# A fused mixture-of-experts and ternary feed-forward block on one core: one-hot tables from ScalarE, a first unit worked in column halves, reordered loads, and one last store

## The reference

```
x = x + tanh(g_xattn) * experts(layernorm(x), token_ids, ctx)
x = x + tanh(g_ffn)   * bitffn(layernorm(x), gate_w, gate_b, val_w, val_b, out_w, out_b)

experts: expert e = min(token_id // 6250, 3) of each row; per row
         y = (silu(h @ ctx[e].T) * (h @ ctx[e].T)) @ ctx[e].T   # one 512x512 matrix per expert, used three times
bitffn:  bit_linear = round(x * 127/max|x|) * max|x|/127  times  clip(round(w/mean|w|), -1, 1) * mean|w|, plus bias
         out = bit_linear(silu(bit_linear(x, gate)) * bit_linear(x, val), out_w)      # 512 -> 2048 -> 512
```

## Time and profile before

| What | us |
|---|---|
| median of 3 runs (309.02 to 309.77) | 309.68 |
| the profiled execution, whole | 310.04 |
| its span on the core | 308.3 |
| TensorE busy | 291.8 (95%) |
| VectorE busy | 261.4 (85%) |
| GpSimd busy | 238.5 (77%) |
| ScalarE busy | 219.2 (71%) |

### The profile page before, as it was taken

One profiled execution on the slowest core, in us unless ns is written; L12 is line 12 of the kernel. 1 busy time (PEld: TensorE's weight loads), 2 busy tenths in 40 slices (PEclk: granted clock), 3 DMA queues, 4 the chain that ended last, 5 costly groups with the idle time before them and its releaser, 6 DMA issues.

```text
span 308.3 us, 5341 instructions
## 1 busy us (share of the span) xinstructions
PE 291.8 (95%) x1438; PEld 141.0 (46%) x1439; DVE 261.4 (85%) x496; ACT 219.2 (71%) x276; POOL 238.5 (77%) x261
## 2 busy tenths in 40 slices
PE   1989999999999999999889999999999999999994
PEld 1445555544444555444334444444444444444453
DVE  5899987787988968679998999999998899888982
ACT  4959686777887746677986796668866876675650
POOL 5656854788888979936678799998989887977863
PEclk9999999999999999999999999999999999999999
DMA  6685798759997873923043635764445423543142
GB/s 261 228 314 202 271 313 305 251 120 307 336 279 189 230 218 102 292 60 109 19 92 72 121 69 119 122 151 88 107 115 119 85 68 86 119 87 82 54 102 105
DMA packets 58902, 49.10 MB, mean 159 GB/s; under 512 B 51135, under 2 KB 51135, under 8 KB 56576
## 3 DMA queue, kind: packets, MB, share of 16 engines
q1 hardware_dynamic: 54304, 35.43, 45.1%
q0 software_dynamic: 4576, 13.40, 12.5%
HBM read 28.35 MB, written 10.00 MB: 124 GB/s over the span
## 4 chain that ended last, share of the span: by engine, by line
PE 83%; DVE 7%; DMA 3%; issue 2%; POOL 2%; ACT 2%; DVEq 0%; POOLq 0%
PE banks L632 27%; PE banks L705 17%; PE banks L726 17%; PE banks L714 16%; PE banks L639 2%; DMA raw<-raw 2%; PE banks L609 1%; DMA xg<-in_x,gather_at 1%; DVE turned L1053 1%; DVE raw L1207 1%; DVE raw L1202 1%; POOL w_both L476 1%; DVE gu_sb L1102 1%; POOL out L548 1%; PE banks L745 1%
## 5 line engine op out<-in xcount | busy, mean ns | idle before, releaser
L476 POOL TENSOR_TENSOR w_both<-raw 128x1024 f32<-128x1024 f32 (+1 forms) x32 | 74.9, 2342 | 7.7 <-DVE raw L1202 6.8
L632 PE MATMUL banks<-w_both,turned 128*128 x348 | 80.0, 379 | 0.6 <-ACT turned L861 0.5
L939 ACT ACTIVATE w_both<-w_both,magic,raw 128x1024 f32 (+1 forms) x31 | 38.2, 1234 | 35.5 <-DVE raw L1221 35.5
L705 PE MATMUL banks<-tern,raw 128*128 128x512 bf16 x256 | 60.5, 379 | 1.6 <-DMA raw<-raw 1.2
L714 PE MATMUL banks<-tern,raw 128*128 128x512 bf16 x256 | 60.5, 379 | 1.3 <-DVE raw L1194 1.3
L726 PE MATMUL banks<-tern,xg 128*128 128x512 bf16 x240 | 56.1, 379 | 0.7 <-DVE raw L1230 0.7
L632 PEld LDWEIGHTS banks<-w_both,turned 128*128 128x128 f16 x348 | 34.0, 98 | 37.5 <-issue 2.3
L1194 DVE SCALAR_TENSOR_TENSOR raw<-banks,raw 128x1024 f32<-128x1024 f32 x32 | 40.8, 1276 | 4.7 <-issue 4.5
L1202 DVE SCALAR_TENSOR_TENSOR raw<-banks,raw 128x1024 f32<-128x1024 f32 x32 | 40.9, 1278 | 3.6 <-PE banks L714 3.6
L1207 DVE TENSOR_REDUCE raw<-w_both 128x1 f32<-128x1024 f32 x32 | 38.8, 1212 | 3.1 <-POOL w_both L476 2.9
L705 PEld LDWEIGHTS banks<-tern,raw 128*128 (+1 forms) x256 | 24.9, 98 | 32.1 <-DMA raw<-raw 1.4
(11 more groups left out here) (134 smaller groups left out, 420.2 us busy)
## 6 DMA issues: line engine op xcount, KB each, us to landing
raw<-in_ctx SPq DMA_DIRECT2D x4, 1024.0 KB, 6.7
raw<-in_L_ffn_gate_w SPq DMA_DIRECT2D x4, 1024.0 KB, 6.8
raw<-in_L_ffn_val_w SPq DMA_DIRECT2D x4, 1024.0 KB, 7.5
raw<-in_L_ffn_out_w SPq DMA_DIRECT2D x4, 1024.0 KB, 6.1
raw<-x_low SPq DMA_DIRECT2D x8, 257.5 KB, 3.5
raw<-x_high SPq DMA_DIRECT2D x8, 257.5 KB, 3.4
raw<-in_L_ffn_gate_b SPq DMA_DIRECT2D x1, 1024.0 KB, 5.4
raw<-in_L_ffn_val_b SPq DMA_DIRECT2D x1, 1024.0 KB, 9.5
```

The lines of the kernel that those rows point to most:

```text
L476: nc.gpsimd.tensor_tensor(z[:, t % 2, 2 * D * c:2 * D * c + width], g_sb[:, c, 0:width], v_sb[:, c, 0:width], ALU.mult).then_inc(z_made, 1)
L632: last = nc.tensor.matmul(acc[:, :], a[:, k * P:(k + 1) * P], flat(w[:, bass.ds(e4 + k, 1), :]), start=(k == 0 and i == 0), stop=(k == KD ...
L705: last = nc.tensor.matmul(ring[pair][:, b, :], flat(xiT[:, bass.ds(t % 2, 1), k, :]), tern[:, k * HC + 2 * c + b, :], start=(k == 0), stop ...
L939: nc.scalar.activation(zq[:, a:b], flat(z[:, bass.ds(t % 2, 1), a:b]), ACT.Identity, scale=flat(sc[:, bass.ds(t, 1), 12:13]), bias=magic[: ...
```

## The change

- One-hot tables: ScalarE spreads `iota_minus` and `iota_id` into two fp16 tables (`minus_rows`, `ids`) while it waits for the weights; their two iotas are made first on GpSimd. VectorE then makes `row_hot` with two `tensor_tensor` compares of 8 columns each on fp16 operands, laid out [place, column], so that a weight load of L595 takes every 16th element. The row number is multiplied into `unit_hot` instead. GpSimd's three compares are gone. The work for `experts_ready` now stands before the wait for the small matmuls.
- Unit 0: normalise, transpose, high half and low half each in two column halves, in two PSUM banks; the first product's first two matmuls need only the first half. `keep_warm(3)` becomes `keep_warm(1)`. ScalarE's second copy of weights comes earlier, since it uses one of those banks.
- SP: weight pieces 8 and 9 are loaded before the DMA transposes start, 10 and 11 behind the first and the third. The biases are loaded when `signed` is 12, not 16.
- Scales: the two x scales become one ScalarE instruction behind `x_round`; z's output scale is made by ScalarE (`out_scale`); z's floor of 1e-5 is a constant column behind z that `z_max` reads, so one VectorE step is gone.
- The end: one store of whole rows in place of two of half rows.

```diff
@@ -29,6 +29,7 @@
+    ZROW = H + 8
...
@@ -39,14 +40,13 @@
-    HOT_DVE = 13
+    HOT = (0, 8, COLS)
-    out_halves = out.rearrange("b s (c d) -> (b s c) d", c=2)
...
@@ -130,7 +129,9 @@
-        row_hot = turned[:, :, :].rearrange("p a b -> p (a b)").rearrange("p (c r) -> p c r", r=P)
+        minus_rows = tern[:, 0:4, :].bitcast(f16).rearrange("p g d -> p (g d)").rearrange("p (r c) -> p r c", c=COLS)
+        ids = tern[:, 4, 0:COLS * UNITS].bitcast(f16).rearrange("p (c u) -> p c u", c=COLS)
+        row_hot = turned[:, :, :].rearrange("p a b -> p (a b)").rearrange("p (r c) -> p r c", c=COLS)
...
@@ -152,7 +153,7 @@
-        x_frees = 6
+        x_frees, bias_frees = 6, 12
...
@@ -160,7 +161,7 @@
-        z = area(2 * H).rearrange("p (b d) -> p b d", b=2)
+        z = area(2 * ZROW).rearrange("p (b d) -> p b d", b=2)
...
@@ -178,6 +179,8 @@
+        first_hT = hT_ps[:, 0:D // 2], guT_ps[:, 0:D // 2]
...
@@ -305,11 +310,14 @@
+            load_weights(8)
+            gathers_landed(10)
+            load_weights(9)
-                if 8 + i < 12:
-                    load_weights(8 + i)
+                if i in (0, 2):
+                    load_weights(10 + i // 2)
...
@@ -321,7 +329,7 @@
-            sp.wait_ge(signed, G)
+            sp.wait_ge(signed, bias_frees)
...
@@ -342,14 +350,15 @@
-                sp.wait_ge(stored[n], 16 * ((TILES - 2 - n) // YS + 1))
-            for n in range(2):
-                sp.wait_ge(stored_last[n], 16)
+                sp.wait_ge(stored[n], 16 * TILES // YS)
+            for ap, pattern, first, step in ((iota_minus, [[-1, P]], 0, 0), (iota_id, [[1, COLS]], 1, COLS)):
+                nc.gpsimd.iota(ap, pattern=pattern, base=first, channel_multiplier=step,
+                               allow_small_or_imprecise_dtypes=True).then_inc(rows_counted, 1)
...
@@ -360,8 +369,7 @@
-            for ap, pattern, first, step in ((iota_unit, [[P, UNITS]], 0, 0), (iota_id, [[1, COLS]], 1, COLS),
-                                             (iota_place, [[P, UNITS]], 0, 1), (iota_minus, [[-1, P]], 0, 0)):
+            for ap, pattern, first, step in ((iota_unit, [[P, UNITS]], 0, 0), (iota_place, [[P, UNITS]], 0, 1)):
...
@@ -476,11 +484,7 @@
-            pool.wait_ge(consts32, 10)
-            pool.wait_ge(rows_named, 1)
-            for c in range(HOT_DVE, COLS):
-                nc.gpsimd.tensor_scalar(row_hot[:, c, :], iota_minus, minus_row[:, c:c + 1], iota_id[:, c:c + 1],
-                                        ALU.is_equal, ALU.mult).then_inc(hot_pool, 1)
+            pool.wait_ge(consts32, 8)
...
@@ -497,6 +501,7 @@
+                    nc.gpsimd.memset(z[:, :, H:H + 1], 1e-5).then_inc(z_floor, 1)
...
@@ -533,21 +538,13 @@
-                pool.wait_ge(o_made, t + 1)
+                pool.wait_ge(o_made, t + 2 if t == TILES - 1 else t + 1)
-            def store_last(c):
-                pool.wait_ge(last_named, 1)
-                pool.wait_ge(o_made, TILES + c)
-                nc.gpsimd.indirect_dma_start(
-                    out=out_halves, out_offset=bass.IndirectOffsetOnAxis(ap=half_row[:, c:c + 1], axis=0),
-                    in_=x1_in[:, (TILES - 1) % XR, c * D // 2:(c + 1) * D // 2], in_offset=None).then_inc(stored_last[c], 16)
...
@@ -568,10 +565,8 @@
-            for t in range(TILES - 4, TILES - 1):
+            for t in range(TILES - 4, TILES):
-            for c in range(2):
-                store_last(c)
...
@@ -588,11 +583,9 @@
-                if c < HOT_DVE:
-                    pe.wait_ge(hot_made, c + 1)
-                else:
-                    pe.wait_ge(hot_pool, c - HOT_DVE + 1)
-                last = nc.tensor.matmul(perm_ps, row_hot[:, c, :], unit_hot[:, c, :],
+                if c in HOT:
+                    pe.wait_ge(hot_made, HOT.index(c) + 1)
+                last = nc.tensor.matmul(perm_ps, row_hot[:, :, c], unit_hot[:, c, :],
...
@@ -629,6 +622,8 @@
+                        if experts == 1 and i == 0 and k == KD // 2:
+                            pe.wait_ge(hThi_made, 1)
...
@@ -661,6 +656,8 @@
+                    elif isinstance(j, int) and j == 0:
+                        pe.wait_ge(hThi_half, 1)
...
@@ -678,11 +675,17 @@
-            turn_h(0)
-            keep_warm(3)
+            for half, made, done in ((0, h_half, hT_half), (1, h_made, hT_done)):
+                pe.wait_ge(made, 1)
+                for k in range(KD // 2):
+                    last = nc.tensor.transpose(first_hT[half][:, k * P:(k + 1) * P],
+                                               h_of(0)[:, (half * KD // 2 + k) * P:(half * KD // 2 + k + 1) * P], ident32[:, :])
+                last.then_inc(done, 1)
+            keep_warm(1)
+                pe.wait_ge(hTlo_half, 1)
...
@@ -804,6 +807,9 @@
+            act.wait_ge(rows_counted, 2)
+            nc.scalar.activation(ids, iota_id.unsqueeze(2).broadcast_to([P, COLS, UNITS]), ACT.Copy).then_inc(tables_made, 1)
+            nc.scalar.activation(minus_rows, iota_minus.unsqueeze(2).broadcast_to([P, P, COLS]), ACT.Copy).then_inc(tables_made, 1)
...
@@ -832,9 +838,9 @@
+            w_copy(1)
-            w_copy(1)
...
@@ -848,6 +854,12 @@
+                    return
+                if j == 0:
+                    for half, done, made in ((0, hT_half, hThi_half), (1, hT_done, hThi_made)):
+                        act.wait_ge(done, 1)
+                        nc.scalar.activation(hT_of(0)[0][:, half * D // 2:(half + 1) * D // 2], first_hT[half], ACT.Copy,
+                                             scale=H_SCALE).then_inc(made, 1)
...
@@ -923,6 +935,8 @@
+                nc.scalar.activation(flat(sc[:, bass.ds(t, 1), 3:5]), gam[:, 0:2], ACT.Copy,
+                                     scale=flat(sc[:, bass.ds(t, 1), 1:2])).then_inc(xs2_made, 1)
...
@@ -938,6 +952,11 @@
+            def out_scale(t):
+                act.wait_ge(zs_made, t + 1)
+                nc.scalar.activation(flat(sc[:, bass.ds(t, 1), 13:14]), flat(sc[:, bass.ds(t, 1), 11:12]), ACT.Copy,
+                                     scale=out_gam[:, 0:1]).then_inc(zs2_made, 1)
...
@@ -966,6 +985,7 @@
+                    out_scale(t - 1)
...
@@ -1007,6 +1028,7 @@
+            out_scale(TILES - 1)
...
@@ -1044,22 +1066,25 @@
-            dve.wait_ge(consts32, 10)
+            dve.wait_ge(consts32, 8)
-                            unit_a.unsqueeze(2).broadcast_to([P, COLS, UNITS]), ALU.is_equal).then_inc(unit_hot_made, 1)
+                            unit_a.unsqueeze(2).broadcast_to([P, COLS, UNITS]), ALU.is_equal).then_inc(units_named, 1)
-            for c in range(HOT_DVE):
-                v.tensor_scalar(row_hot[:, c, :], iota_minus, minus_row[:, c:c + 1], iota_id[:, c:c + 1],
-                                ALU.is_equal, ALU.mult).then_inc(hot_made, 1)
-            dve.wait_ge(perm_done, 1)
-            v.tensor_scalar(gather_at[:, :], perm_ps, -1.0, 0.0, ALU.add, ALU.max).then_inc(gather_ready, 1)
+            dve.wait_ge(tables_made, 2)
+            for n, (a, b) in enumerate(zip(HOT, HOT[1:])):
+                v.tensor_tensor(row_hot[:, :, a:b], minus_rows[:, :, a:b],
+                                minus_row[:, a:b].unsqueeze(1).broadcast_to([P, P, b - a]), ALU.is_equal).then_inc(hot_made, 1)
+                if n == 0:
+                    dve.wait_ge(units_named, 1)
+                    v.tensor_tensor(unit_hot[:, :, :], unit_hot[:, :, :], ids, ALU.mult).then_inc(unit_hot_made, 1)
+            dve.wait_ge(perm_done, 1)
+            v.tensor_scalar(gather_at[:, :], perm_ps, -1.0, 0.0, ALU.add, ALU.max).then_inc(gather_ready, 1)
...
@@ -1079,6 +1104,11 @@
+                if j == 0:
+                    for a, made in ((0, h_half), (D // 2, h_made)):
+                        v.tensor_scalar(h_of(0)[:, a:a + D // 2], unit_rows(0)[:, a:a + D // 2], mean_var[:, n, 0:1], rstd[:, n:n + 1],
+                                        ALU.subtract, ALU.mult).then_inc(made, 1)
+                    return
...
@@ -1093,6 +1123,12 @@
+                if j == 0:
+                    for half, hi_made, made in ((0, hThi_half, hTlo_half), (1, hThi_made, hTlo_made)):
+                        dve.wait_ge(hi_made, 1)
+                        hi, lo = (of[:, half * D // 2:(half + 1) * D // 2] for of in hT_of(0))
+                        v.scalar_tensor_tensor(lo, first_hT[half], H_SCALE, hi, ALU.mult, ALU.subtract).then_inc(made, 1)
+                    return
...
@@ -1180,14 +1216,12 @@
-                v.tensor_scalar(col(t, 3), gam[:, 0:1], col(t, 1), None, ALU.mult).then_inc(xs2_made, 1)
-                v.tensor_scalar(col(t, 4), gam[:, 1:2], col(t, 1), None, ALU.mult).then_inc(xs2_made, 1)
-                    dve.wait_ge(xs2_made, 2 * (t + 1))
+                    dve.wait_ge(xs2_made, t + 1)
...
@@ -1204,22 +1238,19 @@
-                v.tensor_reduce(col(t, 5 + c), z[:, t % 2, 2 * D * c:2 * D * (c + 1)], AX.X, ALU.max,
+                if t == 0 and c == 1:
+                    dve.wait_ge(z_floor, 1)
```

(26 more changed lines are left out.)

8 lines of the change are left out of this document (3 added, 5 removed).

## The result

| | us |
|---|---|
| kernel before, beside the changed one | 309.71 (median of 10, 309.02 to 311.85) |
| changed kernel | 307.97 (median of 10, 307.10 to 309.18) |
| ratio, 95% interval | 0.9928 (0.9907 to 0.9949) |
| the changed kernel's profiled execution | 308.44, span 306.7 |

By the ratio the change makes the kernel 0.72% faster, 2.2 us; 3.6 were predicted. The range of the prediction ended at 307.8: the median lies 0.2 above it, and the ratio, put on the 309.68 that the prediction started from, gives 307.4, inside. Timed again later, the ratio was 0.9946 (0.9915 to 0.9976).

What follows compares the result with a forecast made beforehand. TensorE was taken as the bound, busy all 90 us from 200 to 290, with 3.6 us of waits at the second layer's start. 1.27 + 0.3 + 2.5 - 0.45 = 3.6 gave a median of 306.1, range 304.7 to 307.8.

Steps and rivals of the forecast that it cites:

- Second layer's start: Where the second layer starts: biases and scales remove 2.5 of TensorE's 3.6 us of waits (ends 1.2 and 3.6).
- Head: Start of the kernel up to the first product: tables and column halves together gain 1.27 us.
- The tables' 0.94: Head, VectorE's compares: two 16-bit compares let `gather_at` start at 8.82 instead of 9.76, a gain of 0.94 us.
- all behind `gather_at`, the gathers [...] moves along: Head: the gathers and the fourth expert's load start earlier along with `gather_at`, whose gain is 0.94 us.
- The column halves: Head, unit 0: the product begins 0.5 us earlier, of which 0.33 is taken as gain (ends 0 and 0.5).
- warming ends near 15.4 [...] and costs nothing: Head, TensorE's warming matmuls: they end near 15.4, just when the first half of h is ready, at no cost.
- Rival (d): TensorE's clock: a rise to 2.4 GHz after the warming eats the 3.6 us if slow until 21; 4%.
- rival (c): Units 9 to 16: free transposes also close gaps, 1.2 us instead of 0.3, giving 305.2; 10%.
- SP's order: Expert stage: moving weight pieces 8 to 11 in SP's queue gains 0.3 us (ends -0.4 and 1.2).
- two loads less compete with transposes: Expert stage, SP's queue: fewer loads beside transposes, two more beside gathers; basis of the 0.3 us gain.
- Tail: Behind the last matmul: one whole-row store lands in 2.9 us, a half in 2.4; 0.45 lost (ends 0 and 0.6).
- The 0.78 behind `finish`: Tail: the single last store starts 0.78 us behind the last `finish`, the same moment as before.

Runs made afterwards that it cites:

- e1: Kernel before with only the second layer's edits (scales, constant floor of z, biases at twelve signs): 308.4, ratio 0.9945.
- e12: Kernel before with only the biases issued at twelve signs and the single last store: 309.31, ratio 0.9964.
- e2: Kernel before with only the head's edits (ScalarE tables, two compares, column halves, `keep_warm(1)`): 309.9, ratio 0.9992.
- e6: Changed kernel, unchanged, in a second profiled execution: 309.03, one execution.
- e9: Changed kernel, unchanged, timed again with a third trace: 308.5, 307.33 to 311.65 in twelve.
- e10: Changed kernel in a middle order: piece 8 ahead of the DMA transposes, 9 to 11 behind the first three: 307.54, ratio 0.9912.
- e7: Changed kernel with SP's old order, pieces 8 to 11 each behind one of the first four DMA transposes: 307.77, ratio 0.9889.
- e8: Changed kernel with pieces 8 to 11 loaded only to a quarter, so another output, for timing alone: 307.2, ratio 0.9882.
- e4: Changed kernel with one 256-element memset on GpSimd ahead of its wait for `gather_at`: 307.99, ratio 0.9947.
- e3: Changed kernel with 28 warming matmuls in place of 20: 309.34, ratio 0.998.
- e11: Changed kernel with piece 8 ahead, 9 to 11 behind three transposes, GpSimd memset, warming as 18 plus 2 after an event: 307.57, ratio 0.9895.

## Why the prediction was right in sign and too high

**Second layer's start, predicted 2.5, measured 2.55** in the changed trace and 2.5 in all that have both edits. The split is right too: 1.2 for the DMA wait against 1.36, 1.3 for the scales against 1.16. Of L714's first wait 0.05 was to be left and none was, of L705's 0.5 (0.42), of L714's second 0.6 (0.66), and L726's went in the first trace (0.2 at most in others). e1 and e12 show it by doing it alone.

**Head, predicted 1.27.** This is the step that failed: between 0.1 and 0.4 us at unit 4 where the clock stays up (e2, e6, e9, e10), and a loss of 1.1 to 1.4 where it falls (the first trace, e7, e8). Three terms went wrong. The tables' 0.94 was right up to `gather_at`, but "all behind `gather_at`, the gathers [...] moves along" was not: the three compares taken from GpSimd (L482) had been its last work before the gather, and without them it starts 0.64 us later, shown by e4. The column halves were given 0.33 net, with the product 0.5 earlier: from the landed gather (13.62) the product starts 3.97 us later, against 4.13 before, so 0.16; this term was read from the traces and not run alone. And "warming ends near 15.4 [...] and costs nothing" assumed that the clock rises near 13.5. By the spacing of the matmuls it rises anywhere from about 11.0 (e7) to about 14.1 us (e2), and 20 of them take 5.68 to 7.20 us; with an early rise they end at 14.40 and TensorE stands still. Rival (d) had the clock, but as a rise that comes too late, at 4%; what occurs is a fall. That the pause causes the fall is argued and not shown: the three traces with the long pause are also the three with the earliest rise (20 matmuls in 5.68 to 5.85 us, 6.15 and more elsewhere), and no run has the one without the other. A mean granted clock of 0.995 or less over the span, as in these three traces, stands in 10 of the 63 executions of the kernels with the changed head and 20 warming matmuls (the changed kernel, e2, e4, e6 to e10), in 1 of 12 of e3, and in 3 of 66 of the kernel before that ran beside them; a mean doesn't tell where in the span the clock fell.

**What takes the head's gain.** Even a mended head is worth nothing by unit 12 (e4, e11). Units 9 to 12 take 23.6 to 24.3 us in nine traces and 25.0 to 26.3 in e2, e3, e4, e6 and e11, which all have the new head and an unfallen clock. Of such traces only e9, which had already lost 0.8 at unit 8, and e10 escape. I had looked mainly for a gain there, in rival (c). That the DMA transposes' landing sets that pace is shown for e3 and e6, where TensorE waited 1.4 us for one; e4 and e2 have 0.4 and 0.2 of such waits. In e9 and e11 it is not a transpose but a gather that comes late. TensorE waited 0.8 us (in e9, ahead of unit 8) and 1.3 us (in e11, ahead of unit 11) for VectorE's `gu_sb`, and ahead of that stood VectorE's `bn`, which had waited 0.7 and 1.2 us for a gather to land. VectorE's timeline in e11:

```profile
87.46 0.70 DVE L1122 BATCH_NORM_STATS2 bn<-xg 128x6 f32<-128x512 f32 x1 [1.21 <-DMA xg<-in_x,gather_at]
...
88.28 0.66 DVE L1141 SCALAR_TENSOR_TENSOR gu_sb<-banks,gu_sb 128x512 f32<-128x512 f32 x1
```

The stretch is paced by DMA landings of both kinds. Why they come late in one order and not in the other is shown only in part.

**SP's order, predicted 0.3** (ends -0.4 and 1.2): the sign was most likely wrong. e7, e10 and e11 have another order and the three lowest ratios of the kernels that compute everything, 0.9889 to 0.9912, against 0.9928 and 0.9946. The step at fault is "two loads less compete with transposes": piece 9, moved forward, runs into the first transpose. Issued 1.9 to 2.8 us ahead of it (e3, e4, e6, e9), it makes it take 5.6 to 6.7 us; in the first trace, where the late head put 4.2 us between them, it took 4.1, and without piece 9 ahead 3.1 to 3.4. So an earlier head itself brings the two together. The size, 0.5 to 1 us, rests on medians whose intervals overlap.

**Tail, predicted -0.45, measured +0.2.** The landing was right (2.7 to 2.8 against 2.4, so 0.3 to 0.4 lost), the start wrong. The 0.78 behind `finish` was put down to the wait itself, with the half store in front called hidden. It came from that half store: it issued at 303.71 for 0.96, and the next stood 0.69 behind it, in "issue". With one store the gap is 0.28.

**The sum as it came out.** At the profiled execution: head and experts to unit 18 -1.14, second layer 2.55, tail 0.2, together 1.61, which is the 1.6 between the spans of 308.3 and 306.7. Without the fallen clock the sum is better by what units 9 to 12 leave of it: e9's is -0.65 + 2.55 + 0.2 = 2.1, the measured gain. The parts aren't independent, though. In e2 a kernel that was 1.23 late, with the biases in the old place, had the DMA wait at L705 covered; so some of the lateness would have cost nothing there, and the biases' 1.36 is their worth to a kernel that is on time.

## What to carry to other kernels

A gain on the head of a chain has to be followed engine by engine until it meets a stage that something else paces: here two engines and the DMAs beside units 9 to 12 each took a part, and 0.94 us became nothing. The edits that removed a wait TensorE had once all stages ran (biases, scales) paid in full. Work taken away from an engine may have been what kept it ready; and warming matmuls by count fit only one time of the clock's rise, so let the last of them wait for an event near their use (e11 did, with a pause of 0.68 us; its six executions don't prove the worth of it). And before an SP load is moved forward, look what it will meet.

The two kernels with the middle order (e10, e11) have medians of 307.54 and 307.57, against 308.5 of the changed kernel and 310.65 of the kernel before on the same chip; the intervals of their ratios overlap with the changed kernel's.

## What the runs showed of the hardware

- The granted clock of TensorE fell in each of the three traces in which it stood still for 1.78 to 1.97 us behind the warming, and in none of the ten in which it stood still for 1.41 us or less, nor in e3's, without a pause. The same three had the earliest rise in the warming, so which of the two matters is open. In the first of them it was back at 1.00 by 22 us. Eight matmuls of the product took 3.03 to 3.39 us there and not 1.90.
- GpSimd, after standing still for 6.3 us, started an indirect DMA 0.95 us after its release ended; with a memset 0.84 us ahead, 0.30 (e4, e11).
- The DMA transpose of one unit took 3.0 to 6.7 us with the same bytes, by what was in flight beside it. The Trainium skill (DMA: Bandwidth & Descriptors, Rules for kernel authors) says that DMAs of SP, ScalarE and GpSimd run on the same 16 engines and interleave; the 6.7 us behind a load of 1 MB agree (e6). The load isn't all of it: in e8 one took 6.24 us beside a load of 256 KB.
- Behind one indirect store of half rows GpSimd's next started 0.69 us after its end; behind one of whole rows 0.31 (in e9 the one at 297.49, behind one from 296.13 to 297.18).
